# Two transformer chains on one core: the cross attention turned and copied tile by tile, with turns of one stream between the values of the other

## The reference

```python
q = (xq @ wq).reshape(B, S, N_HEADS, D_HEAD)
k = (xkv @ wk).reshape(B, T, N_HEADS, D_HEAD)
v = (xkv @ wv).reshape(B, T, N_HEADS, D_HEAD)
scale = D_HEAD ** (-0.5)
attn = jnp.einsum('bihd,bjhd->bhij', q, k) * scale
attn = jax.nn.softmax(attn, axis=-1)
out = jnp.einsum('bhij,bjhd->bihd', attn, v).reshape(B, S, D_ATTN)
return out @ wo + bo
```

## Time and profile before

| what | value |
|---|---|
| median of the runs | 2210.88 us (2208.66 to 2211.32) |
| the profiled execution: time, span | 2207.96 us, 2206.2 us |
| PE busy | 2035.3 us (92%) |
| DVE busy | 1129.0 us (51%) |
| ACT busy | 942.3 us (43%) |
| POOL busy | 751.2 us (34%) |
| `cb` of block 0: first turn to the turn of `n9` | 1777.43 to 1801.27 us |
| mean granted clock of PE | 0.97 |

### The profile page before, as it was taken

How to read it: one execution, slowest core, us unless ns; L and a number is a source line. 1 busy time by engine, 2 the same in 40 slices (tenths; PEclk the granted TensorE clock), 3 DMA queues, 4 the chain that set the end, 5 groups by cost and what they waited for, 6 DMA issues and landing times. The chain is left out here.

```text
span 2206.2 us, 26962 instructions
## 1 busy us (share of the span) xinstructions
PE 2035.3 (92%) x10518; PEld 1225.7 (56%) x10558; DVE 1129.0 (51%) x2011; ACT 942.3 (43%) x1443; POOL 751.2 (34%) x504
## 2 busy tenths in 40 slices
PE   5889998798898999999999999999999999999997
PEld 2544444576676754444544454445445866666665
DVE  4667762535445357756455555555553243535353
ACT  5356665333433425555455535553555422222221
POOL 1212200122223126666566656665661011212121
PEclk9999999899998979999999999999999999999999
DMA  7724232000000021100000000000000600000000
GB/s 156 140 32 57 41 49 73 10 1 1 0 1 1 1 65 33 36 1 1 1 1 1 1 1 1 1 1 1 1 1 29 166 9 0 10 1 10 0 10 10
DMA packets 48206, 52.76 MB, mean 24 GB/s; under 512 B 14730, under 2 KB 38988, under 8 KB 47668
## 3 DMA queue, kind: packets, MB, share of 16 engines
q1 hardware_dynamic: 48084, 51.11, 11.0%
HBM read 41.24 MB, written 8.80 MB: 23 GB/s over the span
## 5 line engine op out<-in xcount | busy, mean ns | idle before, releaser
L1847 POOL TENSOR_TENSOR total<-total,pr 128x1024 f32<-128x1024 f32 x183 | 444.4, 2428 | 230.8 <-ACT pr L2057 214.0
L2057 ACT ACTIVATE pr<-sc 128x1024 f32<-128x1024 f32 x256 | 260.0, 1023 | 266.7 <-PE sc L1723 262.1
L1868 DVE TENSOR_REDUCE pmax<-ring 128x1 f32<-128x512 f32 x512 | 314.5, 684 | 98.2 <-PE ring L1671 98.2
L1723 PE MATMUL sc<-q_full,k_full 64*128 64x512 f32 x1024 | 294.9, 589 | 0.0
L1741 PE MATMUL o<-pr,v_pair 128*64 128x512 f32 x1024 | 247.7, 605 | 0.0
L1671 PE MATMUL ring<-k_round,q_round 64*128 64x512 f32 x512 | 214.3, 569 | 5.8 <-DVE k_round L1862 2.0
L632 ACT ACTIVATE probs<-s 128x512 f32<-128x512 f32 (+1 forms) x304 | 157.7, 578 | 96.7 <-PE s L345 58.4
L1032 POOL TENSOR_TENSOR c_scores<-c_scores,c_total 128x1024 f32<-128x1024 f32 (+1 forms) x48 | 77.0, 1616 | 316.6 <-DVE c_total L988 316.6
L466 DVE TENSOR_REDUCE row_max<-s 128x1 f32<-128x1024 f32 (+3 forms) x128 | 124.5, 1018 | 63.5 <-PE s L327 63.4
L1671 PEld LDWEIGHTS ring<-k_round,q_round 64*128 64x128 f32 x512 | 78.5, 189 | 137.5 <-DVE pmax L1868 115.4
L1723 PEld LDWEIGHTS sc<-q_full,k_full 64*128 64x128 f32 x1024 | 128.9, 191 | 25.6 <-issue 16.8
(11 more groups left out here) (344 smaller groups left out, 3495.9 us busy)
## 6 DMA issues: line engine op xcount, KB each, us to landing
qk_dram<-qk_parts SPq DMA_DIRECT2D x32, 192.0 KB, 2.8
q_stack<-qk_dram SPq DMA_DIRECT2D x48, 128.0 KB
k_stack<-qk_dram SPq DMA_DIRECT2D x48, 128.0 KB
x<-in_x SPq DMA_DIRECT2D x4, 512.0 KB, 7.2
region<-in_L_xattn_mlp_w SPq DMA_DIRECT2D x2, 1024.0 KB, 7.1
region<-in_L_xattn_ff_w SPq DMA_DIRECT2D x1, 2048.0 KB, 19.1
out<-region SPq DMA_DIRECT2D x8, 256.0 KB, 2.2
region<-in_L_xattn_sa_wo SPq DMA_DIRECT2D x1, 1024.0 KB, 8.2
```

Source lines behind the costliest of these rows:

```text
L1723: ins = te.matmul(s2[at % 2][:, j], kf[n % 2][head[j], keys], qf[n % 2][head[j], halves[half]], start=False, stop=True)
L1847: pool.tensor_tensor(out=total[half][:], in0=other[:], in1=probs[at % KEPT][:], op=ALU.add).then_inc(sums, 1)
L1868: dve.tensor_reduce(part_max[:, j, t, half:half + 1], ring[bank_of_max(i)][:], AX.X, ALU.max).then_inc(s1_free, 1)
L2057: act.activation(probs[here % KEPT][:], s2[at % 2][:], ACT.Exp).then_inc(s2_free, 1)
```

## The change

Everything is done per tile. PE's turned chunks of one tile now lie together (`turned_of`: tile, then chunk), each tile's turn has its own signal (`turned0`, `turned1`) and its own copy (`turned_kept0`, `turned_kept1`), 1024 columns at a time in `ca` and `cb`, 512 in `cc`. PE's order in `cb` and `cc` is turn (0,0), turn (0,1), values (0,0), turn (1,0), values (0,1), turn (1,1), values (1,0), values (1,1). DVE does top and less of both tiles of a stream, then both sums, before it goes to the other stream. ACT copies tile 0 of stream 0 before the exponentials of stream 1, and tile 1 between them. In `ca` PE's order is unchanged, and its values wait for the second copy. The names in the lists of steps are changed to match. The diff, cut:

```diff
             [Steps(sem(f"{label}_{name}{s}"), [n for n in order if s == (name == "vector") or
-                                               not n.endswith(".turned_kept")]) for s in range(B)]
+                                               ".turned_kept" not in n]) for s in range(B)]
             for name, order in (("tensor", te), ("vector", dve), ("scalar", act), ("gpsimd", pool)))
...
+def turned_of(ch, s, cols):
+    return ch.pT[s][:].rearrange("p c n -> p (c n)")[:, 0:2 * cols].rearrange("p (t c n) -> p t c n", t=2, n=P)
+def cross_turn(te, ch, e, name, i, s, t, cols):
+    after(te, ch.pool[s], f"{name}.probs{t}", i)
+    for c in range(cols // P):
+        ins = te.transpose(ch.ps[s][:, t * cols + c * P:t * cols + (c + 1) * P],
+                           scores_of(ch, s, cols)[:, t, c * P:(c + 1) * P], e.ident[:])
+    ins.then_inc(ch.te[s].sem, ch.te[s].one(f"{name}.turned{t}"))
 def cross_tensor(te, ch, e, name, i, vw, cols, out_bias):
-    def turn(s):
-        for t in range(2):
-            after(te, ch.pool[s], f"{name}.probs{t}", i)
-            for c in range(cols // P):
-                ins = te.transpose(ch.ps[s][:, c * 256 + t * P:c * 256 + (t + 1) * P],
-                                   scores_of(ch, s, cols)[:, t, c * P:(c + 1) * P], e.ident[:])
-        ins.then_inc(ch.te[s].sem, ch.te[s].one(f"{name}.turned"))
-    turn(0)
-    for s in range(B):
-        after(te, (ch.act, ch.dve)[s][s], f"{name}.turned_kept", i)
-        for t in range(2):
-            dst = ch.ps[s][:, t * C:(t + 1) * C]
-            for c in range(cols // P):
-                ins = te.matmul(dst, ch.pT[s][:, c, t * P:(t + 1) * P], vw[:, s, c, :],
-                                start=c == 0, stop=c == cols // P - 1 and out_bias is None)
-            if out_bias is not None:
-                ins = add_bias(te, ch, dst, out_bias)
-            if t == 1:
-                ins.then_inc(ch.te[s].sem, ch.te[s].one(f"{name}.out"))
-            elif s == 0:
-                turn(1)
+    def turn(s, t):
+        cross_turn(te, ch, e, name, i, s, t, cols)
+    def values(s, t):
+        after(te, (ch.act, ch.dve)[s][s], f"{name}.turned_kept{t}", i)
+        dst = ch.ps[s][:, t * C:(t + 1) * C]
+        for c in range(cols // P):
+            ins = te.matmul(dst, turned_of(ch, s, cols)[:, t, c, :], vw[:, s, c, :],
+                            start=c == 0, stop=c == cols // P - 1 and out_bias is None)
+        if out_bias is not None:
+            ins = add_bias(te, ch, dst, out_bias)
+        if t == 1:
+            ins.then_inc(ch.te[s].sem, ch.te[s].one(f"{name}.out"))
+    turn(0, 0)
+    turn(0, 1)
+    values(0, 0)
+    turn(1, 0)
+    values(0, 1)
+    turn(1, 1)
+    values(1, 0)
+    values(1, 1)
...
     return [f"{name}.{x}" for x in ("top0", "less0", "top1", "less1", "total0", "inverse0", "total1", "inverse1",
-                                    "turned_kept")]
+                                    "turned_kept0", "turned_kept1")]
...
-    last = None
     for s in range(B):
...
                               op=ALU.subtract).then_inc(ch.dve[s].sem, ch.dve[s].one(f"{name}.less{t}"))
-            if last:
-                sums(*last)
-            last = (s, t)
-    sums(*last)
-    after(dve, ch.te[1], f"{name}.turned", i)
-    dve.tensor_copy(ch.pT[1][:, 0:cols // P, :].rearrange("p c n -> p (c n)"), ch.ps[1][:, 0:2 * cols]).then_inc(
-        ch.dve[1].sem, ch.dve[1].one(f"{name}.turned_kept"))
+        for t in range(2):
+            sums(s, t)
+    for t in range(2):
+        after(dve, ch.te[1], f"{name}.turned{t}", i)
+        dve.tensor_copy(turned_of(ch, 1, cols)[:, t].rearrange("p c n -> p (c n)"),
+                        ch.ps[1][:, t * cols:(t + 1) * cols]).then_inc(
+            ch.dve[1].sem, ch.dve[1].one(f"{name}.turned_kept{t}"))
...
 def cross_scalar_steps(name):
-    return [f"{name}.exp0", f"{name}.exp1", f"{name}.turned_kept"]
+    return [f"{name}.exp0", f"{name}.exp1", f"{name}.turned_kept0", f"{name}.turned_kept1"]
...
 def cross_scalar(act, ch, name, i, cols):
-    for s in range(B):
-        for t in range(2):
-            after(act, ch.dve[s], f"{name}.less{t}", i)
-            sc = scores_of(ch, s, cols)[:, t]
-            act.activation(sc, sc, ACT.Exp).then_inc(ch.act[s].sem, ch.act[s].one(f"{name}.exp{t}"))
-    after(act, ch.te[0], f"{name}.turned", i)
-    for half in (slice(0, cols // 256), slice(cols // 256, cols // P)):
-        ins = act.activation(ch.pT[0][:, half, :].rearrange("p c n -> p (c n)"),
-                             ch.ps[0][:, 256 * half.start:256 * half.stop], ACT.Identity)
-    ins.then_inc(ch.act[0].sem, ch.act[0].one(f"{name}.turned_kept"))
+    def exp(s, t):
+        after(act, ch.dve[s], f"{name}.less{t}", i)
+        sc = scores_of(ch, s, cols)[:, t]
+        act.activation(sc, sc, ACT.Exp).then_inc(ch.act[s].sem, ch.act[s].one(f"{name}.exp{t}"))
+    def keep(t):
+        after(act, ch.te[0], f"{name}.turned{t}", i)
+        act.activation(turned_of(ch, 0, cols)[:, t].rearrange("p c n -> p (c n)"), ch.ps[0][:, t * cols:(t + 1) * cols],
+                       ACT.Identity).then_inc(ch.act[0].sem, ch.act[0].one(f"{name}.turned_kept{t}"))
+    exp(0, 0)
+    exp(0, 1)
+    keep(0)
+    exp(1, 0)
+    keep(1)
+    exp(1, 1)
...
                     for t in range(2):
-                        after(te, ch.pool[s], f"ca.probs{t}", i)
-                        for c in range(8):
-                            ins = te.transpose(ch.ps[s][:, c * 256 + t * P:c * 256 + (t + 1) * P],
-                                               ch.scores[s][:, t, c * P:(c + 1) * P], e.ident[:])
-                    ins.then_inc(ch.te[s].sem, ch.te[s].one("ca.turned"))
+                        cross_turn(te, ch, e, "ca", i, s, t, 1024)
                 def values(s):
-                    after(te, (ch.act, ch.dve)[s][s], "ca.turned_kept", i)
+                    after(te, (ch.act, ch.dve)[s][s], "ca.turned_kept1", i)
                     for c in range(8):
                         ins = te.matmul(ch.ps[s][32 * (c % 4):32 * (c % 4) + 32, 256 * (c // 4):256 * (c // 4 + 1)],
-                                        e.vcol[:, batch(i), c, :], ch.pT[s][:, c, :], start=True, stop=True)
+                                        e.vcol[:, batch(i), c, :], turned_of(ch, s, 1024)[:, :, c, :], start=True, stop=True)
                     ins.then_inc(ch.te[s].sem, ch.te[s].one("ca.v"))
```

More of the change, by code:

```diff
@@ L1075, in part_chain0 @@
         w = e.w0
-        te_steps = ["n2.T", "ca.q", "ca.scores0", "ca.scores1", "ca.turned", "ca.v", "ca.out", "n3.T", "mlp.up", "mlp.down", "n4.T", "rt.scores",
+        te_steps = ["n2.T", "ca.q", "ca.scores0", "ca.scores1", "ca.turned0", "ca.turned1", "ca.v", "ca.out", "n3.T", "mlp.up", "mlp.down", "n4.T", "rt.scores",
                     "rt.turned", "rt.routed", "n5.T", "gates", "cand"]
```

4 lines of the change are left out of this document (2 added, 2 removed).

## The result

The changed kernel takes **2173.03 us** (median of four runs, 2171.91 to 2174.65) against 2209.93 us before (2208.66 to 2211.32, four runs): ratio **0.9837**, 95% interval 0.9825 to 0.9849. The forecast was 2179 with a range of 2170 to 2194, so it was right in sign and in size, 6 us on the slow side.

The account below looks back on a forecast made before the run. It took the kernel to be bound by PE's matmuls, with PE idle and half clocked in the cross attentions. 21.2 + 5.3 - 1.7 + 6.8 = 31.6 us off the 2210.9 median gives 2179, range 2170 to 2194.

Parts of the forecast that it names:

- `cb`: 21.2 foretold: Four `cb`: values (0,0) start 4.1 us earlier; 4.5 us gained in blocks 0 and 1, 6.1 in 2 and 3.
- The walk: Timeline of `cb`, block 0, instruction by instruction: one 1.1 us wait for POOL, next norm's turn at 1796.7 instead of 1801.27.
- The clock argument: `cb` values: holes of about 2 us halve PE's clock, 1.1 us holes leave it alone; 1.5 of block 0's 4.5 us.
- Rival 1: Half clock stays in each cross attention's values; gain only 18 us, time 2193; chance 0.12.
- Rival 2: Cut batches bring 1.7 us half-clocked stretches at stops, 61 us in all against 32 gained; 2240; chance 0.02.
- The rule that matmuls should come back to back in batches: Skill's warning that TensorE scales power with use; taken strictly, cutting the values' batch keeps the half clock, time 2193.
- `cc`: 5.3 foretold: Four `cc`: DVE's last copy and the next norm come earlier; 5.3 us, bounds 2 and 9.
- `ca`: 6.8 foretold: Four `ca`, 17.4 us each after, DVE's second copy earlier, half clock kept; 6.8 us, bounds 3 and 12.
- "Given back", -1.7: Behind `cc`, PE idles over 1 us longer before the next scores; one further half clock, 1.7 us lost, ends 0 and -5.

Follow-up runs that it names:

- experiment 1: Kernel before, plus five unread products in every `cb` between stream 0's turns and values: 2203.2 us, ratio 0.9973.
- Experiment 2: Changed kernel with ACT's old order, both copies behind all exponentials: 2205.53 us, ratio 0.9978 to the kernel before.
- Experiment 7: Changed kernel plus five unread products between `cc`'s values and the next block's scores, around the norm's second turn: 2170.18 us.
- experiment 4: Changed kernel with PE's order in `cb` and `cc` altered: both value tiles of stream 0 before both turns of stream 1: 2171.65 us.
- experiment 3: Changed kernel with DVE's old order, sums delayed by one tile: 2190.35 us, ratio 0.9916 to the kernel before.
- experiment 8: Changed kernel plus 13 unread products in PE's holes of each `ca`: 2171.22 us, ratio 0.9838 to the kernel before.
- experiment 10: Changed kernel with values first in `cb`, stream 1's turns together in `cc`, and 13 unread products per `ca`: 2164.11 us.
- experiment 11: Changed kernel with values first in `cb` and `cc`, and unread products in `ca`'s holes and before the scores behind `cc`: 2162.97 us.
- experiment 6: Changed kernel with both turns of stream 1 together ahead of values (0,1), in `cb` and `cc`: 2170.65 us, ratio 0.9826.
- experiment 9: Changed kernel with values first in `cb` and both turns of stream 1 ahead of values (0,1) in `cc`, no added products: 2165.99 us.

## Why the prediction was right, step by step

- **`cb`: 21.2 foretold, 21.26 measured.** From turn to turn 19.3 us were foretold and 19.28 came, in all four blocks. The walk holds row by row: POOL's product for (1,0) was to stay 4.81 us behind the first turn and does (1776.68 - 1771.87), DVE's sum (1,0) was to start 3.3 us behind it and starts 3.24. The hole before turn (1,0) shows as 0.78 us instead of 1.1, because the view counts from the end of the bias product; counted as the prediction did, from 3.57 us behind the start of values (0,0), it is 1.05.
- **The clock argument** had two halves. That the holes of 2 + 2.2 us bring the half clock, and at what price, is shown by experiment 1: with the second hole filled and all else in place, the tile of 5.16 or 6.75 us becomes 3.72. Experiment 2 shows it from the other side. That holes of about 1.1 us leave the clock alone was read from `cc` of block 2 only. In blocks 0 and 1 the same holes stood in front of a half-clocked tile, which the argument passed over:

```profile
1856.92 0.66 PE L947 MATMUL c_ps<-ident,c_scores 128*128 128x128 f32 x4 [1.26 <-POOL c_scores L1032]
1858.75 3.46 PE L957 MATMUL c_ps<-vw,c_pT 128*128 128x256 f32 x8 [1.18 <-ACT c_pT L1021]
```

  So this half rested on a chosen row, and the forecast of the full clock was in part luck. What is left after the change is smaller than the 1.1 us it spoke of: one hole of 0.78 us in `cb` and one of 0.7 in `cc`, and the full clock behind them in all eight. Where between these and the holes of before the clock begins to fall is not shown, nor whether turns count as work for it as the added products do. Rival 1 (the clock stays low) is refuted for `cb`: the clock behind the remaining hole is 1.00. Rival 2 (a half-clocked stretch per stop) falls with it, since after the change no `cb` has one. The rule that matmuls should come back to back in batches (the Trainium skill, Perfetto Trace Analysis, Matmul Optimizations) is borne out by experiment 1 as far as it ties what PE is granted to PE's use. Its strict reading as a verdict on this change was wrong: the batch is cut by turns that keep PE busy, and only 0.78 us of hole is left.
- **`cc`: 5.3 foretold, 5.32 measured** (1.78, 1.73, 0.27 and 1.54; foretold 1.7, 1.7, 0.35 and 1.6). The path was the right one: DVE's last copy ends 7.5 us behind the first turn instead of 9.3, and norm and scores follow it.
- **`ca`: 6.8 foretold, 6.5 measured** (4 x 17.4 against 69.93). Turn (0,1) comes 1.86 us behind the first (foretold 1.9) and stream 1's turns 7.50 (foretold 7.6). The half clock stayed, as assumed. The prediction's own figures, 76.3 less 4 x 17.4, give 6.7 and not 6.8, and the rows add up to 76.4.
- **"Given back", -1.7, is the term that failed: it came out at +2.1.** That PE idles longer before the scores is right (2.11 us instead of 1.23 ahead of the norm's second turn). But the half clock does not come on top: it was in three of three blocks before, and it is once in each of them now. It begins earlier, so that part of it is spent in the hole, where it costs nothing, and the way from the scores to the next turn loses 1.0 us instead of 1.7. Experiment 7, where it is 13.8 us at the full clock, gives that price; experiment 4, where it begins later, shows the same stretch at its full one. The step took a wider hole for one more stretch, when the row could only say that there would be one.
- **The parts outside** were costed at nothing and took 1.0 us: 2.4 later at the start of chain 0, which scatters by itself, 1.4 earlier between the chains.
- So the terms miss 2.5 us of the 34.1 by which the profiled executions differ. The rest of the 6 us is in the medians: I put the forecast 2.9 above the profiled execution, as before's stood, and after's median lies 0.8 below its own.

What the prediction did not say is which part would carry this. By experiments 2 to 4 it is ACT's order (32.5 us if undone, 4.4 of them between the chains), then DVE's (17.3), and not the interleaving on PE (-1.4, nothing that the runs can tell).

## What to carry to other kernels

Ask what a copy waits behind on its own queue before asking how fast it is: here two exponentials of the other stream, with their waits for DVE, stood in front of a copy that PE was waiting for, and putting them back there lost nearly all of the gain. Cost a hole twice, once as idle time and once by the granted clock of what follows it; where the hole can't be closed, a few products that nobody reads bought the clock back, but look at the whole program afterwards, since 2.9 of the 5.2 us won in `ca` were lost to the half clock behind `cc` (experiment 8). Choose the order per stage by what is late next: in `cb` that was the next value tile, in `cc` the norm behind DVE's last copy, and giving each its own order gained 7 us more without any added work.

## What was unexpected of the hardware

- Half-clocked stretches move. With `cb` filled, its four went, and in `cc` block 0 lost its own while blocks 2 and 3 got one (first tile 1.99 us before, 3.58 and 2.89 after). With `ca` filled (experiment 8), the scores behind `cc` of block 1 took 16.88 us instead of 15.00. In experiments 2, 10 and 11 two stretches stood between the chains, at 1023 to 1031 and at 1754 to 1762 us, where no instruction had changed; they cost 4.0 to 4.4 us, and what brings them is open.
- The same half clock costs 1.7 us or 1.0 us behind `cc`, by whether it begins in PE's hole or in the scores.
- Holes that left the clock alone measured 0.69 to 0.79 us (behind `cc` in experiments 6 and 9, in `cb` after the change), and in experiment 3 even 1.98 us, a single one between the two turns of `cb`. Behind the holes of 1.97 and 2.11 us ahead of the scores (experiment 4 and the change) it fell in all three blocks. One of 1.23 us there was followed by the half clock in all three blocks before the change, but only in two of three in experiment 1. These are cases with all that stood around them, not a bound.
